# A two-stage cross attention on one core: who goes first in a step, who issues the moves, and one contiguous run per move

## The reference

```
normed = hidden * rsqrt(mean(hidden^2) + 1e-6) * norm_w
q, k, v = normed @ wq, ctx @ wk, ctx @ wv          # 16 heads of 64
attn    = softmax(q @ k^T)                          # no scale
x1      = hidden + (attn @ v, heads joined) @ wo
out     = x1 + softmax(x1 @ ctx^T) @ ctx            # second attention, one head
```

## Time and profile before

| what | value |
|---|---|
| median of 3 runs | 724.87 us (723.35 to 735.34) |
| the profiled execution, its own time | 722.83 us |
| its span (first to last instruction) | 721.1 us |
| TensorE matmul busy | 591.0 us, 82% of the span |
| GpSimd / VectorE / ScalarE busy | 464.6 / 453.3 / 398.4 us (64 / 63 / 55%) |
| mean granted TensorE clock | 0.945 of full speed |
| DMA moved | 94.79 MB, mean 131 GB/s |

### The profile page before, as it was taken

The page is one execution under the profiler, slowest core; times in us unless marked ns, Lnnn a source line. Parts: engine busy times, 40 slices in busy tenths (PEclk is TensorE's granted clock), DMA queues, the critical chain, the costliest instruction groups (busy, mean ns, idle before and its releaser), DMA issues.

```text
span 721.1 us, 10691 instructions
## 1 busy us (share of the span) xinstructions
PE 591.0 (82%) x3664; PEld 528.3 (73%) x3664; DVE 453.3 (63%) x633; ACT 398.4 (55%) x505; POOL 464.6 (64%) x536
## 2 busy tenths in 40 slices
PE   5888688879898889889898789888988698886852
PEld 5777577868787778778787678877877587866842
DVE  3596377676665876667765677677676566664020
ACT  4685446656555666556555656566465556564211
POOL 2147467856687677856587567867597566888301
PEclk9999899989999999989999999999999999999685
DMA  5077537583656656583755665574756555666101
GB/s 182 1 168 173 143 95 162 118 193 89 159 125 151 166 130 157 122 200 72 165 117 139 154 143 133 140 189 105 166 119 148 142 141 129 141 158 143 31 14 33
DMA packets 75711, 94.79 MB, mean 131 GB/s; under 512 B 15210, under 2 KB 73994, under 8 KB 75658
## 3 DMA queue, kind: packets, MB, share of 16 engines
q1 hardware_dynamic: 62986, 78.78, 46.9%
q10 hardware_dynamic: 12672, 15.35, 8.1%
HBM read 8.72 MB, written 0.41 MB: 13 GB/s over the span
## 4 chain that ended last, share of the span: by engine, by line
PE 29%; POOL 26%; DVE 12%; SPq 12%; issue 10%; DMA 5%; ACT 4%; ACTq 1%; POOLq 0%; DVEq 0%
POOL turned_p L504 17%; PE ps_o L1019 14%; SPq L406 10%; DVE neg_max L782 6%; DMA ctx_raw<-in_ctx_dram 4%; PE ps_s L919 4%; PE ps_s L921 3%; PE ps_s L920 3%; POOL c_lo L509 3%; DVE blocks L799 2%; POOL tails L488 2%; PE ps_o L1017 2%; POOL tails L490 1%; ACT probs L597 1%; ACT turned_p L627 1%
## 5 line engine op out<-in xcount | busy, mean ns | idle before, releaser
L504 POOL TENSOR_TENSOR turned_p<-turned_p 128x1408 fp32r<-128x1408 f32 (+1 forms) x113 | 347.4, 3076 | 13.0 <-ACT turned_p L627 13.0
L1019 PE MATMUL ps_o<-turned_p,c_hi 128*128 128x256 f32 (+2 forms) x1296 | 271.1, 304 | 26.8 <-POOL turned_p L504 17.8
L597 ACT ACTIVATE probs<-ps_s,neg_max 128x1444 f32<-128x1444 f32 (+1 forms) x112 | 164.2, 1466 | 174.2 <-DVE neg_max L782 174.1
L782 DVE TENSOR_REDUCE neg_max<-ps_s 128x1 f32<-128x1444 f32 (+1 forms) x112 | 185.4, 1655 | 103.6 <-PE ps_s L921 103.5
L1019 PEld LDWEIGHTS ps_o<-turned_p,c_hi 128*128 128x128 f32 x1296 | 225.1, 202 | 29.9 <-POOL turned_p L504 18.2
L1019 PE MATMUL ps_o<-turned_p,c_lo 128*128 128x256 f32 (+2 forms) x704 | 197.7, 283 | 0.0
L627 ACT ACTIVATE turned_p<-turned_p 128x1536 fp32r<-128x1536 f32 (+1 forms) x113 | 161.2, 1427 | 55.1 <-issue 36.1
L799 DVE STREAM_TRANSPOSE blocks<-probs 128x1408 f32<-128x1408 f32 (+1 forms) x112 | 182.0, 1625 | 0.0
L488 POOL CAST tails<-probs 128x37 fp32r<-128x37 f32 (+1 forms) x224 | 40.9, 215 | 216.5 <-DVE probs L813 216.5
L1019 PEld LDWEIGHTS ps_o<-turned_p,c_lo 128*128 128x128 f32 x704 | 144.6, 205 | 0.0
L919 PE MATMUL ps_s<-cT_hi,q_hi 128*128 128x512 f32 (+3 forms) x312 | 123.9, 397 | 2.0 <-ACT wqk L545 1.5
(11 more groups left out here) (114 smaller groups left out, 419.8 us busy)
## 6 DMA issues: line engine op xcount, KB each, us to landing
turned_p<-blocks SPq DMA_DIRECT2D x680, 96.0 KB, 2.3
turned_p<-blocks ACTq DMA_DIRECT2D x144, 96.0 KB, 2.9
ctx_raw<-in_ctx_dram SPq DMA_DIRECT2D x8, 704.0 KB
turned_p<-blocks SPq DMA_DIRECT2D x56, 48.0 KB, 1.9
turned_p<-blocks ACTq DMA_DIRECT2D x24, 48.0 KB, 2.3
wq_sb<-in_L_xattn_wq_dram SPq DMA_DIRECT2D x2, 256.0 KB, 5.3
wk_sb<-in_L_xattn_wk_dram SPq DMA_DIRECT2D x2, 256.0 KB, 5.5
wv_sb<-in_L_xattn_wv_dram SPq DMA_DIRECT2D x1, 512.0 KB, 6.5
```

Source lines behind the costliest of these rows:

```text
L504: pool.tensor_tensor(lo, lo.bitcast(F32), hi.bitcast(F32), ALU.subtract).then_inc(remainder, 1)
L597: act.activation(probs[step % 2][0:m, 0:S], score_tile(step, m), ACT.Exp, bias=neg_max[0:m, s:s + 1], accum_out=sums[0:m, s:s + 1]).then_i ...
L782: dve.tensor_reduce(neg_max[0:m, s:s + 1], score_tile(step, m), AX.X, ALU.max, negate=True).then_inc(maxed, 1)
L1019: t = pe.matmul(*todo[i], start=(i == 0), stop=(i == len(todo) - 1))
```

## The change

ScalarE's order in a step becomes: round_piece, bank A, one move, exponential, copy_part of the unit that TensorE finishes in the same step, bank B, the rounding of ctx. `HI_LAG` goes from 4 to 5, so the rounding that stood at the end of one step stands at the start of the next. ScalarE issues two moves a group (one in each step) in place of three in one step; SP issues fourteen in place of thirteen. VectorE's order becomes: invert of the step before, maximum, bank A, turn_blocks, take_out of the unit finished in the same step, bank B. The load of ctx is issued at s = 7. In `blocks` and `turned_p` the two items of a group now lie beside each other for each (a, k), so that a move of a full group is 32 runs of 3072 bytes where it was 64 of 1536; with it go the access patterns of rounding, remainder, the narrow products and the multiplication in take_out (its output is now written in another order of its 32-column pieces).

```diff
-    DMA_LAG, HI_LAG, LO_LAG, PV_LAG = 3, 4, 5, 7
+    DMA_LAG, HI_LAG, LO_LAG, PV_LAG = 3, 5, 5, 7
+
+    ACT_MOVES = [(3, 2), (3, 3)]
...
-    LOAD_STEP = 9
+    LOAD_STEP = 7
...
-        blocks = sb("blocks", [P, 2, 2, 4, SLOTS, QD])
+        blocks = sb("blocks", [P, 2, 4, 2, SLOTS, QD])
...
-        MOVES = [(a // 2, a, k) for a in range(4) for k in range(4)]
-
-        ACT_MOVES = [(3, 1), (3, 2), (3, 3)]
-
-        def move(group, piece, a, k):
-            n = number(group)
+        def move(group, a, k):
+
+            t0, nt = tiles(group, a // 2)
+            src = blocks[QD * a:QD * (a + 1), number(group) % 2, k, t0:t0 + nt, :, :]
+            dst = turned_p[QD * k:QD * (k + 1), lo_region(group), 2 * a + t0:2 * a + t0 + nt, :, :]
+            return dst.rearrange("p t s j -> p (t s j)").bitcast(F32), src.rearrange("p t s j -> p (t s j)")
+
+        def of_piece(region, group, piece, n):
+
             t0, nt = tiles(group, piece)
...
+            return turned_p[:, region].rearrange("p (a t) s j -> p a t (s j)", t=2)[
+                :, 2 * piece:2 * piece + 2, t0:t0 + nt, 0:n]
...
-            def spread_rest(group, half):
-                if group is None or half == 1 or tiles(group, 1) is None:
+            def spread_one(group, half):
+                if group is None or tiles(group, 1) is None:
                     return
                 b, g = group
                 n = number(group)
-                act.wait_ge(block_turned, 2 * upto(STEPS * b + 2 * g + 1))
-                if n >= 3:
-                    act.wait_ge(product, last_unit_no(GROUPS[n - 3]))
-                elif n == 2:
-                    act.wait_ge(wvo_ready, 4)
-                for a, k in ACT_MOVES:
-                    act.dma_start(*move(group, 1, a, k)).then_inc(landed[1][n % 2], 16)
+                if half == 0:
+                    act.wait_ge(block_turned, 2 * upto(STEPS * b + 2 * g + 1))
+                    if n >= 3:
+                        act.wait_ge(product, last_unit_no(GROUPS[n - 3]))
+                    elif n == 2:
+                        act.wait_ge(wvo_ready, 4)
+                act.dma_start(*move(group, *ACT_MOVES[half])).then_inc(landed[1][n % 2], 16)
...
             for step in range(TOTAL):
                 b, s = divmod(step, STEPS)
-                unit = finished_at(step)
-                if unit is not None:
-                    copy_part(unit)
...
+                round_piece(*group_at(step, HI_LAG))
                 round_bank(step, "A")
+                spread_one(*group_at(step, DMA_LAG))
                 exponential(step)
+                unit = finished_at(step + 1)
+                if unit is not None:
+                    copy_part(unit)
                 round_bank(step, "B")
...
-                spread_rest(*group_at(step, DMA_LAG))
-                round_piece(*group_at(step, HI_LAG))
...
                 if what == "pair":
                     dve.wait_ge(product_part, dve_count)
                     r0 = P * ITEMS[2 * g]
-                    dve.tensor_tensor(o_norm[:, r0:r0 + 2 * P], ps_o[:, 0, 0:2 * P], o_part[:, :],
+                    a_by_t = [v.rearrange("p (a t j) -> p a t j", a=4, t=2)
+                              for v in (ps_o[:, 0, 0:2 * P], o_part[:, :])]
+                    dve.tensor_tensor(o_norm[:, r0:r0 + 2 * P].rearrange("p (t a j) -> p a t j", a=4, t=2), *a_by_t,
                                       ALU.mult).then_inc(o_normed, 1)
...
             for step in range(TOTAL):
                 b, s = divmod(step, STEPS)
-                unit = finished_at(step)
-                if unit is not None:
-                    take_out(unit)
+                if step:
+                    invert(step - 1)
                 maximum(step)
                 read_bank(step, "A")
                 if step:
-                    invert(step - 1)
                     turn_blocks(step - 1)
+                unit = finished_at(step + 1)
+                if unit is not None:
+                    take_out(unit)
                 read_bank(step, "B")
```

More of the change, by code:

```diff
@@ L94, in landed_value @@
     def landed_value(group, piece):
-        same = [k for k in PIECES if k[1] == piece and number(k[0]) % 2 == number(group) % 2 and k[0] <= group]
+        same = [k for k in GROUPS if number(k) % 2 == number(group) % 2 and k <= group and tiles(k, piece)]
         return 16 * 8 * len(same)
@@ L403, in spread @@
                     sp.wait_ge(xT_copied, 2)
-                for piece, a, k in MOVES:
-                    if tiles(group, piece) is not None and (a, k) not in ACT_MOVES:
-                        sp.dma_start(*move(group, piece, a, k)).then_inc(landed[piece][n % 2], 16)
+                for a in range(4):
+                    for k in range(4):
+                        if tiles(group, a // 2) is not None and (a, k) not in ACT_MOVES:
+                            sp.dma_start(*move(group, a, k)).then_inc(landed[a // 2][n % 2], 16)
             for step in range(TOTAL):
@@ L495, in take_remainder @@
                     return
[L496 to L502, removed]
+                lo = of_piece(lo_region(group), group, piece, FULL * QD)
+                hi = of_piece(hi_region(group), group, piece, FULL * QD)
                 pool.wait_ge(rounded, pieces_to(group, piece))
@@ L617, in round_piece @@
                 n = number(group)
[L618 to L622, removed]
                 act.wait_ge(landed[piece][n % 2], landed_value(group, piece))
@@ L626, in round_piece @@
                     act.wait_ge(product, last_unit_no(GROUPS[n - 2]))
-                act.activation(part(hi_region(group)), part(lo_region(group)).bitcast(F32), ACT.Copy)\
+                act.activation(of_piece(hi_region(group), group, piece, RUN),
+                               of_piece(lo_region(group), group, piece, RUN).bitcast(F32), ACT.Copy)\
                     .then_inc(rounded, 1)
@@ L792, in turn_blocks @@
                 m = QD * quadrants(item)
-                dst = blocks[0:m, n % 2, t, :, :, :].rearrange("p k s j -> p k (s j)")
+                dst = blocks[0:m, n % 2, :, t, :, :].rearrange("p k s j -> p k (s j)")
                 if n >= 2:
@@ L997, in products @@
                 else:
-                    t0, nq = (0, 4) if what == "late" else (4, 2)
+                    t, nq = (0, 4) if what == "late" else (1, 2)
                     w = QD * nq
@@ L1004, in products @@
                     for j in range(FULL):
[L1005 to L1008, removed]
+                        todo += [(both, c_hi[cp][:, j, :], turned_p[:, at:at + by + 1:by, t:t + 2 * nq:2, j, :]),
+                                 (own, c_lo[cp][:, j, :], turned_p[:, hi, t:t + 2 * nq:2, j, :])]
+                    todo.append((own, c_hi[cp][:, FULL, :], turned_p[:, hi, t:t + 2 * nq:2, FULL, :]))
+                    rinv = (ps_o[:, 0, 2 * w:3 * w], rinv_ones[:, :], turned_p[:, hi, t:t + 2 * nq:2, FULL, :])
                 cut = [len(todo) * k // parts for k in range(parts + 1)]
```

## The result

The changed kernel takes 630.06 us (median of 4 runs, 627.58 to 633.31), the kernel before 727.94 us beside it. The ratio is 0.868, 95% interval 0.860 to 0.875: 13% faster. Ratios compare only executions in the usual state; in a few others the same kernel ran at a lower granted clock and some per cent longer, so a ratio need not be the quotient of the medians beside it. The forecast was 663 us, the range 635 to 696.

A forecast was written before the change was run, and what follows sets the result against it. TensorE's waits, chiefly for GpSimd's remainder (a loop through VectorE's maximum) and the ctx load, were taken to bound the kernel. 33 + 11 + 25 + 13 - 20 = 62 us off 722.8 gave 661, as median 663 us; range 635 to 696.

The forecast's parts named there:

- VectorE inverts first: Reciprocal ahead of VectorE's maximum: shortens the loop through GpSimd, cutting TensorE's 43.0 us of remainder waits to 10; gain 33.
- take_out last, copy before the rounding: VectorE's and ScalarE's order: of TensorE's 18.9 us of waits for what VectorE takes out, 8 stay; gain 11 us.
- ctx two steps sooner: Load of ctx on SP: lands over 6 us early, so all 25.0 us of TensorE's waits for it go.
- the rival: Only the late load helps, as the loop closes again: 25 us and 13 of clock, 38 together, 687 us; chance 0.16.
- The move to SP and the new waits: SP nearly full, VectorE's bank steps, ScalarE's landings: 2.7 us of new waits per batch, 20 us charged.
- Bank steps, landings and take_out: Per batch, 1.2 us for VectorE's bank steps and 0.5 for ScalarE's rounding meeting landings; 8 us of take_out waits kept.
- a sign of being wrong: VectorE's transposes waiting for landings in most groups, or ScalarE's rounding waiting for the DMA, would show the forecast wrong.
- The clock: TensorE's granted clock, 0.96 in the steady part, loses 20.6 us; with less idle time 8 stay lost; gain 13.
- TensorE is left as the only bound: Without the 20 us of new waits and with 5 more of clock: 638 us; chance 0.20.
- Only the late load goes: Loop closes again through SP and landings or VectorE's bank steps; gain 25 and 13 of clock, 687 us; chance 0.16.
- ScalarE's order closes the loop: ScalarE's rounding, first in its step, waits for the landing and delays exponential and reciprocal: 715 us; chance 0.08.
- the long runs make the issue dear: SP's issues would take 0.90 us each with longer runs and set the pace: 792 us, slower; chance 0.04.

The follow-up runs named there:

- undo_invert_first: The changed kernel with VectorE's reciprocal back behind the maximum and bank A: 684.67 us, ratio 0.943 to the kernel before.
- undo_take_out_last: The changed kernel with copy_part back at the head of ScalarE's step, ahead of the rounding, and take_out ahead of VectorE's maximum: 628.83 us, ratio 0.868.
- undo_long_runs: The changed kernel with the old layout of blocks and turned_p, 64 runs of 1536 bytes per move: 636.88 us, ratio 0.882.

## Why the prediction was wrong in size, point by point

The steady part gave 603 - 516 = 87 us and the tail behind it 71.1 - 64.8 = 6.3, together the 93.3 us between the spans. The forecast had 62 and 0.

- **VectorE inverts first (33 us): right.** The loop was the right one; undo_invert_first brings it back to within 0.02 us. That what is left (10.9 us in 11 waits) is so near to what was left standing (10) is in part luck. Six of the waits, 5.0 us, lie where the prediction put them, behind the low part of ctx, but they are shorter than it had them. The other five, 5.9 us, lie in the first batch, before 100 us.
- **take_out last, copy before the rounding (11 us): right in size, wrong in cause.** The prediction had take_out in the maximum's way and costed the two orders apart. undo_take_out_last shows that take_out ahead of the maximum costs nothing once the loop is open and the copy is ahead of the rounding. What counts is the copy ahead of the rounding: 0.868 against 0.920 when both orders are undone, 5% or 38 us. The prediction saw the rounding ahead of the copy in the earlier trace rows and didn't follow it to the next product; in the kernel before, the longer loop through GpSimd hides it.
- **ctx two steps sooner (25 us): right.** 1.1 us is left. Alone, the edit is worth 4.6%, 34 us, where the rival put 38.
- **The move to SP and the new waits (20 us): this step failed.** The charge was 2.7 us a batch: 1.0 for SP, and 1.2 for steps with a bank and 0.5 for landings, together 12.6 us over 7.4 batches, beside the 8 us of waits for take_out that were kept. By the kernel with 12 issues, whose SP has time to wait, the two parts came out in opposite ways.
  - *Bank steps, landings and take_out: 20.6 us charged, 2.4 measured.* That kernel's 9.9 us of idle time are 7.5 for the remainder and 2.4 for everything else. The lateness of take_out in steps with a bank was charged twice, as part of the 8 and as part of the 1.2, and each wait on the way was taken for a wait at TensorE's end. In the changed kernel VectorE did wait 24.4 us for landings, and ScalarE's rounding 14.8 us (12 times), which the prediction had named as a sign of being wrong; yet TensorE's waits that were not there before are only the two for cT_lo, 1.5 us in all. A likely reason is the lead: TensorE's scores need the exponential of two steps before, and its products what was rounded a step before. No run varies that lead.
  - *SP: 7.4 us charged, 11 us of idle time measured, and 5 of busy time besides.* Little of it stands under a name of its own in TensorE's list. With 14 issues the first and later products wait 5.8 us for take_out, with 12 issues 1.7 (47 to 547 us). The 64.8 us a batch that the prediction gave SP left out the long issues. From the first scores of the third batch (157.2 us) to those of the eighth (500.9) a batch takes (500.9 - 157.2)/5 = 68.7 us, and in that stretch SP waits 1.4 us in all, so its own work takes 68.5 a batch. 28 of its 840 DMA issues take over 1 us (294.72 in the chain above), and what all of them take beyond 0.6 us adds up to 28.0 us, 3.5 a batch, about the difference. TensorE has 65.5 to 68.1 us of work a batch at full clock, so the slower of the two sets the pace, now one, now the other.

  The Trainium skill (DMA: Bandwidth & Descriptors, section on issuing engines) calls the time to issue usually small beside the DMA. In this kernel it is not: 0.59 us for an issue against 2.2 to its landing, and 65 us of the whole for two issues a group.
- **The clock (13 us): right.** By the prediction's formula 20.6 us were lost before and 516 x 0.01 x 0.96 = 5 now, so 15.6 came back. The formula takes TensorE to be half as fast at the lower level. In the trace of before the product's matmuls start every 0.21 us there (from 380 us on) and every 0.12 at full clock, so the loss is a little smaller than that. With 12 issues the clock is 1.00 from 45 to 560 us.
- **Left out: what a wait costs besides its length.** TensorE's busy time fell by 515.7 - 495.1 = 20.6 us, 7.6 more than the 13 that were forecast, and the clock explains at most 15.6 of it. The rest, 5 us or more, was taken as fixed. An estimate from the traces comes near: a product's matmul has a record of 0.28 us, but in a run of them the next one starts 0.12 after it, and only the last before a wait is covered by nothing. TensorE stands idle 63 times in the steady part before and 32 times after: 31 x 0.16 = 5 us. No run tests this.
- **Left out: the tail (6.3 us).**

Sum of the differences: idle time 66.4 in place of 49 (17), busy time 20.6 in place of 13 (8), tail 6: 31 us, which is what lies between 62 and 93.

Of the rivals, "TensorE is left as the only bound" (638 us, chance 0.20) was nearest: VectorE, ScalarE and GpSimd at 80, 68 and 83% of the steady part, where the prediction had feared 85 to 95, and a fourth queue that is nearly full still let TensorE reach 96% of it (495.1/516). It is not the only bound, since SP is beside it. "Only the late load goes", "ScalarE's order closes the loop" and "the long runs make the issue dear" are out: the issue takes 0.59 us with runs of 3 KB.

## What to carry to other kernels

When a chain of waits shows a loop, write down the next shortest loop too: a part of the change that does nothing in the kernel before, or when undone alone, may be what opens that second loop, and only both orders undone at once show it. A wait on an engine that runs a step or more ahead need not be a wait at TensorE: charge it only by what goes beyond that lead, and only once. Count the queue that issues DMAs like an engine, by issues times their spacing plus its long ones, and leave it some slack: here one issue in fourteen fewer was enough.

## What was not expected of the hardware

- SP's issues are not all alike: 0.59 us in the median, but 28 of the changed kernel's 840 take 1.0 to 1.8 us, one about every 19 us. In the kernel before it is 22 of 784, 1.1 to 2.0 us, one about every 28 us. What these are was not tried.
- ScalarE's single issue in a step takes 0.51 us with one run per partition (the changed kernel) and 0.59 with two (undo_long_runs, which differs from it in the layout alone). On SP, the first issue of a group is also the shorter one in the changed kernel (0.53 in the median), and those right behind it take 0.59; with two runs the two are 0.59 and 0.60. So the gain of a long run shows mainly in an issue that follows a pause.
- Runs of twice the length hardly moved faster. A packet of 1536 bytes on SP's queue took 0.107 us in the mean, one of 3072 bytes 0.203: 14 and 15 GB/s.
